# First batch's value projection between the prologue's maximum tiles, second batch's sigmoid behind four exponentials

## The reference, cut to what matters

```
x = layernorm(x + gated_linear_attention(x))      # 16 heads, decay gates, silu output gate
x = layernorm(x + cross_attention(x, ctx))        # Q from x, K and V from ctx, 16 heads of 16
x = layernorm(x + ffn(x))                         # r = sigmoid(..), k = relu(..)^2

V      = (ctx @ W_v)                              # the value projection of this case
scores = Q K^T / 4 ;  attn = softmax(scores) ;  out = attn V ;  out @ W_o + b_o
gate   = silu(x @ Wg + bg) = z * sigmoid(z)       # the sigmoid of this case
```

## Time and profile before

| | before |
|---|---|
| median of 3 runs | 558.35 us (556.93 to 558.68) |
| the profiled execution, its own time | 558.42 us |
| its span, first to last instruction | 556.6 us |
| mean granted TensorE clock | 0.942 of full speed |
| TensorE busy | 476.6 us, 86% |
| VectorE busy | 386.5 us, 69% |
| ScalarE busy | 294.2 us, 53% |
| GpSimd busy | 218.5 us, 39% |

### The profile page before, as it was taken

The page is one execution under the profiler, slowest core; times in us unless marked ns, Lnnn a source line. Parts: engine busy times, 40 slices in busy tenths (PEclk is TensorE's granted clock), DMA queues, the critical chain, the costliest instruction groups (busy, mean ns, idle before and its releaser), DMA issues. The chain is left out here.

```text
span 556.6 us, 6300 instructions
## 1 busy us (share of the span) xinstructions
PE 476.6 (86%) x1979; PEld 200.1 (36%) x1979; DVE 386.5 (69%) x635; ACT 294.2 (53%) x516; POOL 218.5 (39%) x214
## 2 busy tenths in 40 slices
PE   8997889879877878999878788979998797888984
PEld 3433424314221113454333233533342252233553
DVE  4988879566676885477987977598457838632275
ACT  4144430744564745536687638347855515487334
POOL 5569794530378771423588663321000101000000
PEclk9999989989797979999999999998989988798898
DMA  7566451422765303025753021211421100000011
GB/s 218 183 195 168 138 144 45 108 58 66 189 162 132 96 1 96 19 68 161 177 142 77 24 64 45 83 28 30 116 58 27 44 25 2 1 0 3 0 39 38
DMA packets 24832, 45.49 MB, mean 82 GB/s; under 512 B 4672, under 2 KB 15584, under 8 KB 24800
## 3 DMA queue, kind: packets, MB, share of 16 engines
q1 hardware_dynamic: 21680, 38.02, 24.9%
q10 hardware_dynamic: 3120, 7.08, 5.2%
HBM read 34.93 MB, written 9.96 MB: 81 GB/s over the span
## 5 line engine op out<-in xcount | busy, mean ns | idle before, releaser
L1435 DVE TENSOR_REDUCE MX<-bank 128x1 f32<-128x512 f32 x256 | 166.6, 681 | 117.8 <-PE bank L587 112.9
L1060 ACT ACTIVATE PT<-bank 128x512 f32<-128x512 f32 x256 | 147.0, 597 | 128.1 <-PE bank L596 118.6
L587 PE MATMUL bank<-KS,QS 96*128 96x512 bf16 x240 | 94.4, 401 | 39.7 <-DVE MX L1435 30.3
L596 PE MATMUL bank<-QS,KS 99*128 99x512 bf16 x256 | 100.6, 404 | 15.5 <-ACT PT L1060 15.0
L610 PE MATMUL bank<-PT,Vs 128*32 128x512 f32 x512 | 78.5, 689 | 1.5 <-ACT PT L1060 0.8
L1747 POOL TENSOR_TENSOR W<-qT,W 128x512 f32<-128x512 f32 x48 | 61.6, 1287 | 38.9 <-DVE W L1354 26.7
L596 PEld LDWEIGHTS bank<-QS,KS 99*128 99x128 bf16 x256 | 24.4, 99 | 108.0 <-issue 59.3
L587 PEld LDWEIGHTS bank<-KS,QS 96*128 96x128 bf16 x240 | 23.8, 99 | 100.3 <-DVE MX L1435 64.2
L1733 POOL TENSOR_TENSOR W<-kT,W 128x512 f32<-128x512 f32 x32 | 46.3, 1451 | 6.7 <-ACT kT L918 6.7
L1778 POOL TENSOR_TENSOR MP<-MX,zero 128x16 bf16<-128x16 f32 x15 | 4.4, 291 | 113.0 <-DVE MX L1435 73.2
L1354 DVE TENSOR_TENSOR_SCAN W<-bank,W 128x512 f32<-128x512 f32 x32 | 38.7, 1209 | 0.0
(11 more groups left out here) (216 smaller groups left out, 719.1 us busy)
## 6 DMA issues: line engine op xcount, KB each, us to landing
W<-v_rows SPq DMA_DIRECT2D x12, 512.0 KB, 6.4
W<-v_rows ACTq DMA_DIRECT2D x12, 512.0 KB, 6.5
k_parts<-parts SPq DMA_DIRECT2D x24, 128.0 KB, 2.4
KS<-k_parts SPq DMA_DIRECT2D x16, 192.0 KB, 3.5
q_parts<-parts SPq DMA_DIRECT2D x24, 128.0 KB, 2.5
QS<-q_parts SPq DMA_DIRECT2D x16, 192.0 KB, 3.6
cT<-in_cT SPq DMA_DIRECT2D x4, 512.0 KB, 3.6
xtok<-in_x SPq DMA_DIRECT2D x4, 512.0 KB, 5.1
```

The source lines that it names most:

```text
L587: pe.matmul(bank(n)[:, :], QS[0:NS, h, i * P:(i + 1) * P], KS[0:NS, h, :], start=True, stop=True).then_inc(filled(n), 1)
L596: pe.matmul(bank(name)[:, :], KS[0:NR, h, kt * P:(kt + 1) * P], QS[0:NR, h, :], start=True, stop=True).then_inc(filled(name), 1)
L1060: act.activation(PT[:, n % 2, j, :], bank(name)[:, :], ACT.Exp).then_inc(emptied(name), 1)
L1435: dve.tensor_reduce(MX[:, NT * h + i:NT * h + i + 1], bank(n)[:, :], AX.X, ALU.max).then_inc(emptied(n), 1)
```

## The change

The values of batch 0 move into the prologue: the new `first_values(n)` issues one product of V0 or V1 (a quarter of each) in place of the filler behind each of the first eight maximum products. The fillers behind the other eight stay. ScalarE copies the values ahead of the row of maxima, and batch 1's sigmoid moves from there to behind the fourth exponential of step 0. The other batches' values stay where they were.

```diff
--- before.py
+++ after.py
@@ -80,6 +80,7 @@
     ("gy0", 0, 4), ("gy1", 0, 1), ("K1", 0, 2), ("gt0", 0, 5), ("gt1", 0, 3), ("Q0", 0, 6), ("Q1", 0, 1),
     ("gz0", 1, 5), ("gz1", 1, 2), ("o0", 1, 0),
     *((f"m{h}.{i}", 0, 3 + i % 2) for h in range(4) for i in range(NT)), ("mr0", 0, 3), ("o1", 1, 0),
+    ("V0", 0, 2), ("V1", 0, 1),
 ]
 
 EARLY_SCANS = 11
@@ -140,7 +141,7 @@
                     use("decay", r, 2)
                 if (n, i) in SIDE_USES:
                     name, which, bank = SIDE_USES[n, i]
-                    if (which, stage[which]) != ("f", LAST):
+                    if (which, stage[which]) != ("f", LAST) and (s, which) != (0, "b"):
                         use(name, stage[which], bank)
                 for which, h, tile in MAXIMA[s].get((n, i), []):
                     use(f"m{h}.{tile}", stage[which], 3 + tile % 2)
@@ -708,6 +709,17 @@
                 ins = pe.matmul(bank("var", 0)[:, :], mavg[:, :], sq[:, k, :], start=(k == 0), stop=(k == 1))
                 if k == 1:
                     ins.then_inc(filled("var", 0), 1)
+
+            def first_values(n):
+
+                m, half, k = n // 4, n // 2 % 2, n % 2
+                tt = 2 * m + half
+                if n % 4 == 0:
+                    pe.wait_ge(*free_for(f"V{m}", 0))
+                ins = pe.matmul(bank(f"V{m}")[:, half * D:(half + 1) * D], cT[:, k, tt * P:(tt + 1) * P], xwv[:, k, :],
+                                start=(k == 0), stop=(k == ND - 1))
+                if n % 4 == 3:
+                    ins.then_inc(filled(f"V{m}"), 1)
 
             def first_max(h, i):
                 if i == 0 and h % 4 == 0:
@@ -793,7 +805,10 @@
                 for h in range(4):
                     for i in range(NT):
                         first_max(h, i)
-                        keep_busy("s0.0", 0, 1)
+                        if h < 2:
+                            first_values(NT * h + i)
+                        else:
+                            keep_busy("s0.0", 0, 1)
                     if h == 1:
                         reduce_four(1, 1)
                 keep_busy("s0.0", 0, 6)
@@ -874,7 +889,7 @@
                             feed_forward(f, (n, i))
                         if b == LAST and (n, i) in FIRST_SUMS:
                             first_sums(FIRST_SUMS[n, i])
-                        if b is not None and n == 0 and i < 2:
+                        if b and n == 0 and i < 2:
                             by_token(f"V{i}", b, cT, xwv, i)
                         for which, h, tile in MAXIMA[s].get((n, i), []):
                             if stage[which] is not None:
@@ -1051,6 +1066,15 @@
                 act.activation(mrow[:, :], bank(f"mr{g}")[0:48, 0:P // 2].bitcast(BF16), ACT.Copy).then_inc(emptied(f"mr{g}"), 1)
                 act.wait_ge(*read(f"mr{g}", b))
                 act.dma_start(QS[NS:NR, 4 * g:4 * g + 4, :], mrow[:, :]).then_inc(m_in, 16)
+
+            def values_set(b):
+                for m in range(2):
+                    act.wait_ge(*full_of(f"V{m}", b))
+                    if b:
+                        act.wait_ge(pv_done, count(H, b, 0))
+                    act.activation(Vs[:, 2 * m:2 * m + 2, :, 0:HD],
+                                   bank(f"V{m}")[:, :].rearrange("p (t h e) -> p t h e", t=2, e=HD),
+                                   ACT.Copy).then_inc(emptied(f"V{m}"), 1)
 
             def exp_tile(b, n, j):
                 name = f"s{n}.{j}"
@@ -1261,8 +1285,8 @@
                 act.wait_ge(r_done, count(RQ, 1, 2))
                 act.wait_ge(*full_of("gy1", 0))
                 act.activation(oS[:, 0, :], bank("o0", 1)[:, :], ACT.Copy).then_inc(emptied("o0", 1), 1)
+                values_set(0)
                 max_rows(0, 0)
-                first_sigmoid(1)
 
             prologue()
             for s in STEPS:
@@ -1281,17 +1305,14 @@
                             gated_end(o, (n, i))
                         if b is not None:
                             exp_tile(b, n, i)
+                        if s == 0 and (n, i) == (0, 3):
+                            first_sigmoid(1)
                         if (n, i) in ROWS and stage[ROWS[n, i][0]] is not None:
                             max_rows(stage[ROWS[n, i][0]], ROWS[n, i][1])
                         if i == 2 and group[0] is not None:
                             invert(*group)
-                        if n == 0 and i == 3 and b is not None:
-                            for m in range(2):
-                                act.wait_ge(*full_of(f"V{m}", b))
-                                act.wait_ge(pv_done, count(H, b, 0))
-                                act.activation(Vs[:, 2 * m:2 * m + 2, :, 0:HD],
-                                               bank(f"V{m}")[:, :].rearrange("p (t h e) -> p t h e", t=2, e=HD),
-                                               ACT.Copy).then_inc(emptied(f"V{m}"), 1)
+                        if n == 0 and i == 3 and b:
+                            values_set(b)
             tail()
```

## The result

The changed kernel takes 558.64 us (median of 20 runs, 552.71 to 560.9), the kernel before 555.67 us in its 20 runs beside it (551.99 to 558.68). The ratio is 1.0047, 95% interval 1.0026 to 1.0068: slower, by 2.6 us (1.4 to 3.8). Its profiled execution took 560.71 us, span 558.9, mean clock 0.929 against 0.942. The forecast was 559.7, +1.3 on the three runs of before that were known then; over 20 runs that kernel's median is 2.7 us lower. One execution of experiment e5, which took 1541.83 us, is left out of its ratio; all others of this document lie between 549 and 563 us.

The account below looks back on a forecast made before the run. A chain of waits over TensorE, VectorE and ScalarE was taken to bound the kernel, locally GpSimd's last product. +1.21 - 0.79 + 0.71 + 0.2 = +1.3 us on 558.35 gave 559.7; range 556.1 to 561.3.

Parts of the forecast that it names:

- loop, GpSimd's product, gap, low clock: Prologue to step 0: loop later by 1.21 us, product 15 ending near 99.8, TensorE idle about 3.5, clock then 0.50.
- rival C: Downstream of the shift: one more low-clock stretch costs up to 1.6 us, +2.9 in all, 561.3 us; chance 0.18.
- Loop, +1.21: Maximum loop: eight value products replacing eight fillers, partly at the low clock, delay everything behind it by 1.21 us.
- V0, V1 and the third score, -0.79: Step 0: the last head sum stops waiting for the third score but still waits for GpSimd's product; gains 0.79 us, not 3.46.
- rival B: Last head sum: GpSimd doesn't hold it, so V0 and V1 count in full; -2.25 us, 556.1 us; chance 0.17.
- ScalarE, GpSimd, SyncE at nothing: Moved copies, sigmoid, later gate work and context load cost nothing, hidden by idle time or, for the context, by 0.5 us.
- rival A: Ahead of K0: no clock drop or its cost hidden; +0.42, or up to +0.8 through the context's landing; chance 0.17.
- The clock, +0.9: Behind TensorE's idle gap: halved clock costs +0.71 us on the last head sum and +0.2 on the way to K0.
- Sum: Whole kernel: +1.21 - 0.79 + 0.71 + 0.2 = +1.3 us, predicted as 559.7 us; chance 0.48.

Follow-up runs that it names:

- e5: e4 with batch 1's context sent behind V1, ahead of the keys and queries of the last two groups; ratio 0.9989 to the kernel before.
- e4: e3 with batch 0's value products moved out of the maximum loop, in place of the fillers behind it; ratio 1.0000 to the kernel before.
- e3: The changed kernel with 14 fillers ahead of the last head sum of batch 1; ratio 1.0003 to the kernel before.
- e1: The kernel before with only batch 1's sigmoid moved behind the fourth exponential of step 0; ratio 1.0011 to the kernel before.
- e7: The changed kernel once more, unaltered, for a second trace; single execution, 562.21 us.
- e8: The kernel before once more, unaltered, for a second trace; single execution, 558.36 us.
- e6: e5 with batch 1's last head sum moved behind the next quarter's maxima, 10 fillers in its old place; 552.28 us, ratio 0.9971 to the kernel before.
- e9: The kernel of e6 again, for a second interval and trace; 553.55 us, ratio 0.9977 to the kernel before.
- e2: The changed kernel with batch 1's sigmoid back in ScalarE's prologue, so only the values move; ratio 1.0068 to the kernel before, 3.8 us slower.

## Why the prediction was right, and where it was off

**Sign and mechanism.** The steps came out in the order given: loop, GpSimd's product, gap, low clock. The kernel is slower, as forecast, and the time lies inside the range. The size is that of rival C (+2.9), and like C it comes of more low time than the forecast's 3.4 us, but at the forecast's own place and not at a late point further down.

**The number, and luck.** That 559.7 lies so near the measured 558.64 is luck in part: it was built on 558.35 for the kernel before, whose median over 20 runs is 555.67. The change was forecast at +1.3 and is twice that, +2.6 (1.4 to 3.8), and over its base the range reached no further than +2.9. A change within 0.3%, not told from none, had the largest chance, 0.57; the measured one is 0.47% and clear of noise, for which the prediction gave 0.26.

**Loop, +1.21.** Measured +1.32, and e4 against e3 gives 1.37. **V0, V1 and the third score, -0.79.** The last head sum starts 22.60 us behind the first maximum product against 22.05, so +0.55 with the loop's +1.32: -0.77. GpSimd's product 15 does bound it, and rival B falls: TensorE waited 3.42 us for it.

**ScalarE, GpSimd, SyncE at nothing.** Right in the changed kernel (e1 for the sigmoid). But the landing that rival A named is real: where the clock stays up, K0 waits for it (e1, e3, e4), and it takes all that e1 gained. e5 takes it away. The prediction had put its latest time too early, at 3.8 us behind the issue; it was 4.2 to 4.4 in e1 to e4, e7, e8 and the changed kernel.

**The clock, +0.9: the term that was mis-sized.** It measures +2.79 from the head sum's start to K0 in the changed kernel. I had taken one low stretch of 3.4 us that begins about when the work does, with +0.71 on the head sum and +0.2, at most 1.0, on the rest. The low stretch was 10.2 us in both traces and covered the whole way to K0. The head sum alone lost 0.86, the way from there to the value row another 0.89, value row to K0 another 1.04: 1.93 on the rest. The 3.4 us came from two low stretches of one trace, and the length at one and the same place varies: the second of them, 119.5 to 122.9 in the kernel before, lasted from 119.4 to 126.2 in e8, which is the same kernel. Without the clock's term the sum would have been +0.42, and what is left of the ruler without it is +0.55. I had also argued that maxima and scores at VectorE's pace would lose little. At 0.50 a score and a maximum need 0.83 us (101.26 to 102.09) while VectorE needs 0.6 for the maximum, so TensorE became the pace-maker. Rival A falls as to the clock: with the 3.4 us gap it dropped in both traces; with the gap filled, in none of e3 to e6 and e9 between 83 and 116 us.

**Sum.** +1.32 - 0.77 + 2.79 = +3.34 in the ruler, +2.3 in the spans and +2.6 (1.4 to 3.8) in the timed runs. Downstream of K0 the spans are 451.7 and 451.2 us before and after, but 445.7 in e3, whose trace has less low time there, and 445.5 to 448.1 in e4, e5, e6 and e9. The timed runs don't bear such a saving out: e3's ruler is 1.7 us longer than that of before, and its time 0.2 us more (-1.5 to +1.8), where 4 us less would have been due. So a single span proves little within 6 us, and the ruler was the better witness. Why just these five traces are short there stays open.

**Slips in the prediction.** The gaps that rival A calls rows 1 are in the earlier trace rows, and VectorE sets the loop's pace from the second pair of heads on (there are two). Neither enters the sum.

**Open.** Why the clock stayed at 0.50 for 8.3 us of unbroken work here, and rose after 3.4 us in the maximum loop, no run settles. Nor was it tried how few fillers would do.

## What to carry to other kernels

Moving work off an engine at a place where it waits for another one doesn't shorten the wait, it only empties it; on TensorE the emptied wait can cost more than the work did, because the clock falls (here 2.79 us, where the work's leaving gave 0.77). Look for where a wait is bounded from (here GpSimd's last product), put the moved work into stretches that are already filled with dummies for such a wait, and read, before a gain is booked, which transfer lands just behind the point that moves. For a change of a microsecond, measure the distance between two instructions in the traces and not the whole time.

## What the runs showed of the hardware

A gap of 3.4 us on TensorE (0.28 us of work in 95.7 to 99.1) was followed by a granted clock of 0.50 for 10.2 us in two traces of two, and one of 4.3 us by 6.8 us of it in e2. Work at the low clock didn't lift it soon: TensorE was busy in 3.40 of 3.40 us from 101.1 to 104.5 and still at 0.50 until 107.9. The same place of the same kernel had a low stretch of 3.4 us in one trace and of 6.8 in another (119.5 us on, before and e8). The low stretch behind the 2.1 us gap ahead of the maximum loop came in nine traces of eleven but not in e5 and e6, the order of work in the loop being that of e9, where it came; it is worth 0.9 us there. Batch 1's context, 512 KB, landed 3.8 to 4.4 us behind its issue when it was queued behind twelve loads of keys and queries, and 3.3 to 3.6 us behind it when it was issued ahead of them (e5, e6, e9).
